# Gate spreading in a fused attention and mixture kernel: 128-row matmuls against 64-row tiles in pairs

## The reference, cut to what matters

```python
x = x + _L0_conv_ref(_ln_c(x), ...)   # 8x8 window attention, 4 heads of 16
t = _to_tokens(x)                     # 64 numbers a token
t = t + _L0_ffn_ref(_ln_t(t), router_w, router_b, expert_w, expert_b)
# in _L0_ffn_ref, for 8 experts, the 2 best of each token:
router_probs = jax.nn.softmax(x @ router_w + router_b, axis=-1)
top_p, top_i = jax.lax.top_k(router_probs, K)
top_p = top_p / jnp.sum(top_p, axis=-1, keepdims=True)
expert_out = jnp.einsum('bnd,edc->bnec', x, expert_w) + expert_b
```

## Time and profile before

| what | value |
| --- | --- |
| median of 3 runs | 1270.95 us (1270.83 to 1271.89) |
| profiled execution, its own time | 1268.81 us |
| span in its profile | 1267.0 us |
| TensorE matmul busy | 1192.4 us, 94% |
| VectorE, ScalarE, GpSimd busy | 1053.9 us, 920.4 us, 1081.7 us |
| DMA queue, share of 16 engines | 27.6% |

### The profile page before, as it was taken

One profiled execution on the slowest core, in us unless ns is written; L12 is line 12 of the kernel. 1 busy time (PEld: TensorE's weight loads), 2 busy tenths in 40 slices (PEclk: granted clock), 3 DMA queues, 4 the chain that ended last, 5 costly groups with the idle time before them and its releaser, 6 DMA issues.

```text
span 1267.0 us, 47630 instructions
## 1 busy us (share of the span) xinstructions
PE 1192.4 (94%) x19840; PEld 729.4 (58%) x19840; DVE 1053.9 (83%) x2247; ACT 920.4 (73%) x1743; POOL 1081.7 (85%) x925
## 2 busy tenths in 40 slices
PE   4579999999999999999999999999999999999986
PEld 3456666655565666656566666655556565666531
DVE  6458898888888889898888888988888888888874
ACT  6368778867777887877677888777767776777742
POOL 6368999989888999999988899998988888888753
PEclk9599999999999999999999999999999999999998
DMA  7012333322223233322222333332222222222221
GB/s 203 5 38 66 92 94 86 81 61 71 55 60 81 77 90 94 91 59 61 70 55 62 95 88 86 88 87 55 58 65 66 53 65 65 63 56 66 64 70 42
DMA packets 95622, 91.43 MB, mean 72 GB/s; under 512 B 26928, under 2 KB 62384, under 8 KB 95408
## 3 DMA queue, kind: packets, MB, share of 16 engines
q1 hardware_dynamic: 95408, 88.37, 27.6%
HBM read 35.90 MB, written 17.83 MB: 42 GB/s over the span
## 4 chain that ended last, share of the span: by engine, by line
PE 67%; DVE 10%; POOL 7%; DMA 7%; issue 5%; ACT 5%; SPq 0%; DVEq 0%; POOLq 0%; ACTq 0%
PE bank_y L530 16%; PE bank_s L410 8%; PE bank_t L425 8%; PE bank_s L384 6%; PE bank_o L464 4%; PE bank_g L518 4%; DMA r_b<-recip_rows 4%; PE bank_o L438 4%; PE bank_p L454 4%; PE bank_p L518 3%; DVE t_g L992 3%; DMA recip_rows<-r_out 2%; PE bank_t L394 2%; PE bank_y L502 2%; DVE prob L880 2%
## 5 line engine op out<-in xcount | busy, mean ns | idle before, releaser
L1142 POOL TENSOR_TENSOR t_g<-t_t,g_copy 128x512 f32<-128x512 f32 x192 | 245.6, 1292 | 72.0 <-ACT g_copy L712 70.8
L530 PE MATMUL bank_y<-t_g,w_exp 128*64 128x512 f32 x1024 | 268.9, 616 | 6.7 <-DVE t_g L992 4.7
L1120 POOL TENSOR_TENSOR prob<-prob,mx 128x512 f32<-128x512 f32 x256 | 261.8, 1045 | 14.7 <-DVE mx L887 14.5
L675 ACT ACTIVATE prob<-prob 128x512 f32<-128x512 f32 x256 | 159.4, 623 | 128.6 <-POOL prob L1120 128.6
L992 DVE TENSOR_TENSOR t_g<-t_t,bank_p 128x512 f32<-128x512 f32 x256 | 174.2, 680 | 9.2 <-PE bank_p L518 7.3
L880 DVE TENSOR_TENSOR prob<-bank_s,rel 128x1024 f32<-128x1024 f32 x128 | 156.3, 1221 | 28.4 <-PE bank_s L410 23.7
L425 PE MATMUL bank_t<-idn,prob 128*128 128x128 f32 x1024 | 163.6, 283 | 5.5 <-ACT v_bd L670 5.0
L679 ACT ACTIVATE prob_t<-bank_t 128x512 f32<-128x512 f32 x256 | 152.5, 596 | 21.3 <-PE bank_t L425 21.2
L712 ACT ACTIVATE g_copy<-bank_g 128x512 f32<-128x512 f32 x192 | 113.8, 593 | 74.1 <-PE bank_g L518 73.9
L425 PEld LDWEIGHTS bank_t<-idn,prob 128*128 128x128 f32 x1024 | 112.8, 141 | 79.2 <-issue 65.9
L887 DVE TENSOR_REDUCE mx<-prob 128x16 f32<-128x1024 f32 x128 | 155.4, 1214 | 2.2
(11 more groups left out here) (122 smaller groups left out, 2345.1 us busy)
## 6 DMA issues: line engine op xcount, KB each, us to landing
t_t<-t_rout SPq DMA_DIRECT2D x256, 128.0 KB, 2.4
x_in<-in_x SPq DMA_DIRECT2D x68, 256.0 KB, 3.3
r_b<-recip_rows SPq DMA_DIRECT2D x64, 256.0 KB
out_y<-y_out SPq DMA_DIRECT2D x128, 128.0 KB, 2.6
r_in<-sum_b SPq DMA_DIRECT2D x64, 16.0 KB
recip_rows<-r_out SPq DMA_DIRECT2D x64, 16.0 KB, 1.7
t_g<-in_sel SPq DMA_DIRECT2D x1, 512.0 KB, 3.6
rel<-in_relb SPq DMA_DIRECT2D x1, 256.0 KB, 2.9
```

The source lines that it names most:

```text
L530: mm(B_Y[C * a:C * a + C, :], w_exp[:, pair, :], t_g[:, (2 * pair + a) % TG, :], start=False, stop=(pair == MIXES // 2 - 1), skip_group_ch ...
L675: A(prob[:, i], prob[:, i], ACT.Exp).then_inc(p_ready.sem, 1)
L1120: G.tensor_tensor(sc, sc, mx[:, i, :].unsqueeze(2).broadcast_to([P, 2 * HEADS, NTOK]), ALU.subtract).then_inc(s_shifted.sem, 1)
L1142: G.tensor_tensor(t_g[:, u % TG, :], t_t[:, p, u % 2, :], g_copy[:, n, :], ALU.mult).then_inc(tg_pool.sem, 1)
```

## The change

The parts of the gates are put in other places: `GATE_PARTS` is now 0, 1, 2, 0, 1, 2, 0, 1, so that places 0 to 3 (rows 0 to 63 of `g_t`) and places 4 to 7 (rows 64 to 127) each hold all three parts. VectorE's steps 16, 18 and 19 write every third place, and `BIAS_PARTS` is changed to match. The selection matrices of even gates have their ones in rows 0 to 63 only, those of odd gates in rows 64 to 127 only. The matmul of gate u contracts over these 64 rows, so its array shape is 64x128, and even and odd gates use different halves of the array. In TensorE's order gate 2 goes behind the turned logits, directly ahead of gate 3, and gate 5 goes ahead of transposes 3, directly behind gate 6. Gates 4 and 7 stay where they are.

```diff
--- before.py
+++ after.py
@@ -52,8 +52,9 @@
 SQUARES, PLANES, SCALES = range(3)
 CHUNK = 32
 PARTS = 3
-GATE_PARTS = (0, 0, 0, 1, 1, 1, 2, 2)
-BIAS_PARTS = (0, 1, 2, 0, 1, 2, 0, 1)
+GATE_PARTS = (0, 1, 2, 0, 1, 2, 0, 1)
+BIAS_PARTS = (0, 0, 0, 1, 1, 1, 2, 2)
+SEL_PARTS = ((0, 1, 2), (4, 5, 6))
 STAGES = ("project", "attend", "output", "route", "mix")
 LN_C_EPS, LN_T_EPS = 1e-6, 1e-5
 
@@ -515,7 +516,8 @@
                     pe.wait_ge(g_copied.sem, g_copied.at(g, ON_POOL.index(u - 2) + 1))
                 elif u:
                     pe.wait_ge(tg_dve.sem, tg_dve.at(g, ON_DVE.index(u - 2) + 1))
-                mm(B_GATE[u % 2][:, :], gate_sel16[:, u, :], g_t[:, :], start=True, stop=True
+                rows = slice(C * (u % 2), C * (u % 2) + C)
+                mm(B_GATE[u % 2][:, :], gate_sel16[rows, u, :], g_t[rows, :], start=True, stop=True
                    ).then_inc(gate_done[u % 2].sem, 1)
 
             def experts(g, pair):
@@ -561,11 +563,10 @@
                     logits(j - 2)
                 if attending and work.take:
                     turn_probs(j, 1, work)
-                if mixing:
-                    gates(j - 3, 2)
                 if routing_on:
                     turn_logits(j - 2)
                 if mixing:
+                    gates(j - 3, 2)
                     gates(j - 3, 3)
                 if projecting:
                     project(j + 1, QUERIES)
@@ -581,12 +582,10 @@
                     take(work.batch, *work.take, 1, j)
                 if mixing:
                     experts(j - 3, 1)
-                if mixing:
                     gates(j - 3, 6)
+                    gates(j - 3, 5)
                 if attending:
                     turn_probs(j, 3, work)
-                if mixing:
-                    gates(j - 3, 5)
                 if outputting:
                     project_out(j - 1)
                 if projecting:
@@ -976,13 +975,13 @@
                     elif step == 15:
                         V.tensor_tensor(gates, hot, over_experts(share), ALU.mult).then_inc(route.sem, 1)
                     elif step == 16:
-                        V.tensor_copy(g3[:, :, 0:3, :], thrice(by_pair[0], 3)).then_inc(route.sem, 1)
+                        V.tensor_copy(g3[:, :, 0::3, :], thrice(by_pair[0], 3)).then_inc(route.sem, 1)
                     elif step == 17:
                         V.tensor_tensor(by_pair[1], by_pair[0], g3[:, :, 0, :], ALU.subtract).then_inc(route.sem, 1)
                     elif step == 18:
-                        V.tensor_copy(g3[:, :, 3:6, :], thrice(by_pair[1], 3)).then_inc(route.sem, 1)
+                        V.tensor_copy(g3[:, :, 1::3, :], thrice(by_pair[1], 3)).then_inc(route.sem, 1)
                     elif step == 19:
-                        V.tensor_tensor(g3[:, :, 6:8, :], thrice(by_pair[1], 2), thrice(g3[:, :, 3, :], 2), ALU.subtract).then_inc(route.sem, 1)
+                        V.tensor_tensor(g3[:, :, 2::3, :], thrice(by_pair[1], 2), thrice(g3[:, :, 1, :], 2), ALU.subtract).then_inc(route.sem, 1)
 
             def gate(g, p, u):
                 dve.wait_ge(gate_done[u % 2].sem, gate_done[u % 2].at(g, u // 2 + 1))
@@ -1220,7 +1219,7 @@
     for g in range(2):
         bexp[:, g, :, g, :] = a["eb"]
         for e in range(EXPERTS):
-            sel[[0, 3, 6], g, e, e // 2 * 2 + g, e % 2, :] = 1.0
+            sel[list(SEL_PARTS[g]), g, e, e // 2 * 2 + g, e % 2, :] = 1.0
     kmask = np.zeros((2, HEADS, DH, 2), f)
     kbias = np.zeros((2, HEADS, DH, 2), f)
     for h in range(HEADS):
```

## The result

The changed kernel takes 1279.4 us (median of 4 runs, 1278.9 to 1281.9) against 1271.4: a ratio of 1.0068, with a 95% interval of 1.0052 to 1.0084, so it is slower by 0.7%. The profiled execution took 1279.08 us with a span of 1277.3, 10.3 us more than before in both.

A forecast was written before the change was run, and what follows sets the result against it. TensorE was taken as the bound: 39 slots without intake at +0.28 us and 24 with intake at +0.15 make 14.5, less 2.8 taken up elsewhere, +11.7; with 2.1 from profiled execution to median, 1282.6 us, range 1263 to 1292.

The forecast's parts named there:

- (1): Gates 0 and 1 as a pair: 0.17 us less on TensorE, but waited for behind ScalarE's token copy: 0.
- (2): Gate 2 moved behind the turned logits, paired with gate 3: turned logits to projection 0.66 for 0.53, +0.13 us.
- (3): Gate 4 stays alone; the transposes before it now leave their array shape: +0.09 us.
- (5): Gate 7 alone, behind the turned values: a change of array shape, +0.09 us.
- (4): Gate 5 moved to gate 6: gate 6 to output projection 0.94 for 0.97, -0.03 us.
- (6): Gate parts stored at every third place by VectorE: taken as 0, or some tenths of a microsecond per slot.
- with intake: 24 slots that also turn new input planes: +0.15 us each, the second block of experts held by VectorE's product of gate 3.
- What other chains take up: A quarter of the 39 slots without intake was taken to absorb the addition in other waits: 2.8 us less.
- Rival B: Faster: changing rows alone needs no drain, so the five new boundaries cost nothing; 1265 us, chance 0.17.
- C: Pairs of gates don't overlap in the 64x128 shape: 17 us more, 1300 us, chance 0.07.
- E: Everything saved on TensorE comes back: 42 us, 1229 us, chance 0.02.
- D: Shape changes drain TensorE, but other chains take up nearly all in both slot kinds: about no change, 1272 us, chance 0.06.

The follow-up runs named there:

- the repeat: The changed kernel run once more, unaltered, for a closer interval and more executions of its end: ratio 1.0075 to the kernel before.
- tiles-alone run: The change without its order: every gate on 64 rows, gates 2 and 5 in their old places; ratio 1.0259 to the kernel before, 1303.5 us.
- gates 4 and 7 back: The changed kernel, but the lone gates 4 and 7 go over all 128 rows; ratio 1.0019 to the kernel before, 1272.8 us.
- storage alone: New places of gate parts and new selection matrices, but all gates over 128 rows in the old order; ratio 0.9995 to the kernel before, 1269.9 us.
- order alone: The change with every gate over all 128 rows, gates 2 and 5 still moved; ratio 1.0029 to the kernel before, 1274.8 us.
- early queries on 128 rows: The kernel before with the queries' projection ahead of the turned logits, gate 2 behind them, all gates over 128 rows; ratio 0.9951, 1264.8 us.

## Why the prediction was right

It gave 1282.6 us, +11.7; measured were +8.0 at first and, in the repeat, +10.2 (both by the medians). By its steps:

- (1) right. Logits 1.34 behind the tokens' transposes as before; the run with the first pair on 128 rows lost nothing.
- (2) right in kind, +0.09 for +0.13: turned logits to projection 0.62 for a forecast of 0.66. The turned logits reach the pair in 0.26 (1089.73 to 1089.99) and not in 0.30. Behind that two errors cancel: the second gate of a pair costs 0.01 and not 0.05, but it waits 0.05 for the product of gate 1, where I had set 0.04 at most and taken 0. GpSimd's product of gate 2 starts 0.33 later against the logits (forecast 0.30), and that cost nothing in this slot.
- (3), (5) right: transposes to gate 4 0.59, 0.10 more than before; undone, the two gave back about 6 us.
- (4) 0.91 for 0.94: -0.06, not -0.03, again since the second gate costs nothing.
- (6) right, measured at zero.
- Slots: 18.18 for a forecast of 18.23; with intake +0.15 as forecast, and held by VectorE as described.
- The sum went wrong in two places that offset each other, which is luck. What other chains take up was a choice of mine, 2.8 us; it was about 6 of the 13 that the steps add up to with their measured sizes (39 x 0.24 + 24 x 0.15), because 23 of the 36 middle slots without intake had such a wait, not a quarter. And the end of the span was not in the sum at all; there the profile shows 3.5 us more. Of the 10.3 us in the profiled executions the slots that the steps speak of make up only 6.7.

Rival B falls with the 0.59 before gate 4 and with the tiles-alone run: a change in rows alone costs the same 0.10, so the rule of the Trainium skill (TensorEngine Tiling (Array Packing), Key Properties) that a change of tiling mode drains TensorE is borne out for 64x128 too, as far as a price can show it. C falls with the starts 0.00 to 0.01 apart. E falls with the run of gates 0, 1, 4 and 7 on 128 rows. D had a part of the truth: over the 23 slots with waits the addition was taken up almost whole, but not in the steady ones.

## What to carry to other kernels

Putting two 64-row matmuls side by side is worth one matmul (0.22 us here) only where TensorE would otherwise work, and each boundary to blocks of another array shape takes back 0.10, or 0.15 where the weights of the next block had loaded early; count the boundaries in the order of issue before counting the pairs, and leave a lone small matmul in the shape of its neighbours. A matmul that stands in a wait is free: moving it out to pair it makes it cost, and the better use of the wait was a longer block (1264 us). When a gain of 0.55 us in a slot comes out as a third, look for the next waits in the same slots, here GpSimd's and the reciprocals' DMA. And before an operation is moved into a wait, see that the wait is there in every kind of slot: in six slots GpSimd had none, and the move cost there most of what it gained elsewhere.

## What the hardware showed that was not expected

Where it waits for nothing, the second matmul of a pair starts 0.00 to 0.01 us after the first, and the pair costs no more than a lone gate on 64 rows (0.32 to the next block in both).

The weights of a block load ahead of its first matmul only if the block before has the same array shape. In the kernel before, between 128x128 blocks, the load of transposes 3 starts at 350.74 for a first matmul at 350.95, and over the trace such a load starts up to 0.22 us ahead; behind a change of shape it is never more than 0.03, in the repeat of the change as well. Those transposes reach gate 5 in 0.44; transposes 2, with a change of shape ahead of them, reach gate 4 in 0.49.

Kernels with six or eight gates over 64 rows ran at a lower mean granted clock: 0.976 (the change, ten executions), 0.977 (tiles alone, four) and 0.977 (gates 4 and 7 back, twelve), against 0.980 before (75). With one or two pairs and the rest over 128 rows it was 0.978 to 0.981. In the profiles of the change and of the kernel before the difference lies mostly in the last 50 us, where TensorE has gaps of 1 to 2 us. The clock there was 0.76 in both profiles of the change and in that of the tiles alone, 0.90 to 0.96 in three kernels with 128-row gates (the kernel before, storage alone, order alone), but 0.85 in another (early queries on 128 rows). These are single executions, and 64-row gates as the cause are not shown.
